# The last two stages of a four-layer gated block: first loads issued a stage earlier, first norms in the tail, statistics in eights

## The chip, the core and the metric

The kernel runs on one core of a Trainium2 chip. A core has five engines that matter here: TensorE (PE, matrix products and transposes into PSUM), VectorE (DVE), ScalarE (ACT), GpSimd (POOL) and SyncE (SP), which here only issues transfers. Each runs its own list of instructions in order and waits for others on semaphores. The metric is the device time of one execution in microseconds (us); lower is better.

## The reference, cut to what matters

`x` is 32 batches of 112 rows of 256. Four layers follow each other, each of an attention over a context of 375 rows and of a feed-forward part, both gated by a tanh and added to `x`. The change touches the last three parts: the ternary layer of layer 2, the masked attention and the routed layer of layer 3.

```python
# x (32, 112, 256), ctx (32, 375, 256), mask (32, 112, 375) of 0 and 1
x = x + tanh(g_ffn[2])   * ternary(_layernorm(x), ternary_weight, bias, act_scale)
x = x + tanh(g_xattn[3]) * masked(_layernorm(x), ctx, ctx, mask, gamma, beta)
x = x + tanh(g_ffn[3])   * routed(_layernorm(x), router_w, router_b, expert_weights)

def masked(q, k, v, mask, gamma, beta):
    logits = einsum('bsd,btd->bst', q, k) / sqrt(256)
    logits = where(mask == 0, -9e15, logits)
    x = einsum('bst,btd->bsd', softmax(logits), v)
    return _layernorm(x) * gamma + beta

def routed(tokens, router_w, router_b, expert_weights):       # 8 experts, the best 2 are used
    probs = softmax(einsum('bsh,eh->bse', tokens, router_w) + router_b)
    top_p, top_i = top_k(probs, 2)
    w = top_p / (sum(top_p) + 1e-10)
    y_all = einsum('nh,ehd->ned', tokens, expert_weights)      # every expert for every row
    return sum of w * y_all[top_i], divided by the clipped sum of w
```

## The kernel before

All of `x` stays in SBUF (`x_sb`) from the first layer to the last; the layers are blocks that follow one another, and at the end of a block every engine waits for the others. In the trace the ternary layer lies at 2764.9 to 2835.2 us, the masked attention at 2835.2 to 2960.4 and the routed layer at 2960.4 to 3235.7. The order of the instructions on each engine is written out by hand.

**Ternary layer** (`ternary_layer`, L2735). SP issues eight blocks of the context, `ctx_sb`, for the next stage (L2755) and has nothing else to do there.

**Masked attention** (`masked_attention`, L622 on). One pass of the loop for each of 32 batches, and three more to drain. PE: two transposes of the normed `x` (`transpose_xn`, L854), two matmuls with the transposed context `ctx_t` (`scores`, L864), three transposes of the probabilities two passes later (L873) and three matmuls with the context (`attend`, L884). ACT: copy of `xn_t` (L806), copy of `probs_t` (L820), the mask made into a summand (`add_mask`: `size` L795, `add` L799), the exponentials (L812), and the load of a context block whose buffer is free (`load_ctx`, L825); its list starts with the loads of gamma and beta. DVE: norm of the batch four ahead (L727), `kept` (L736, scores plus summand), `probs` with the top of a row (L740), statistics, and the adds to `x_sb` (L760). POOL: gain (L703), normalisation of the output and beta. SP: masks for two batches at a time in three buffers (L668), `ctx_t` in four buffers (L673), late in the stage the eight matrices of experts (`we`, L681). At the end POOL raises the variances of the first eight batches plus epsilon to the power -1/2 (`routed_scales(0)`, L568) and with that the block ends. `load_ctx` also runs for the last eight batches, which reload context blocks 0 to 7 that nobody reads.

**Routed layer** (`routed_layer`, L2866 on). The batches are routed in three groups, 0 to 7, 8 to 15 and 16 to 31 (`ROUTES`). For a group: statistics of `x` (`routed_statistics`, L550 and L553), rstd on POOL (`routed_scales`), norm on DVE (L2924) into eight buffers `xn`, two transposes on PE (L3042), copy on ACT (L3031), two matmuls with the router (L3053) and `route_group` on DVE, some 24 small instructions that choose the two experts and their weights. Then for each pair of batches PE runs 16 matmuls with a 128x512 operand (32 records in the trace) (`experts`, L3065) into five banks of PSUM, and DVE adds each result, weighted, to `x_sb` (`add_experts`, L2992). What DVE and PE do for the next group is written between the pairs of the present one: statistics after pair 0 of a group, eight norms after the second, the other eight norms (if there are sixteen) and `route_group` after the third; PE has its transposes and logits after the second pair, and the second eight after the third.

## Time and profile before

| | us |
|---|---|
| median of three runs | 3272.77 |
| lowest and highest of them | 3262.78, 3273.53 |
| the profiled execution | 3237.5 |
| its span | 3235.7 |
| granted clock over the span, share of full | 0.96 |
| masked attention | 125.2 |
| routed layer | 275.3 |

PE is busy for 94% of the span, DVE 62%, ACT 45%, POOL 19%. The rows are in the section below, taken from three views: the table by stretches (busy time of each engine in a stretch), and the timeline (one line for a run of like instructions of one engine, with start, busy time, and in brackets the longest wait ahead and what ended it). In names of tiles `ps` is PSUM.

### The profile page before, as it was taken

What the parts mean: (1) busy time and instruction counts of PE and PEld (TensorE: products, weight loads), DVE (VectorE), ACT (ScalarE), POOL (GpSimd) and SP (SyncE); (2) the same over time, 40 slices, a digit from 0 to 9 for tenths busy, and PEclk for the clock granted to TensorE, in tenths of its full rate; (3) what the DMA queues carried; (4) which work ended last, traced back from release to release, by engine and by line L of the source; (5) the groups of instructions that cost most, each with busy time, mean ns of one, the idle gap of its engine ahead of it and who ended that gap; (6) DMA issues with size and microseconds to landing.
All of it is one profiled execution on the core that took longest, in us unless ns stands there. A gap on an engine that the chain in (4) does not pass through costs nothing. (4 is left out here: it accounts for less than half of the span.)

```text
span 3235.7 us, 61226 instructions
## 1 busy us (share of the span) xinstructions
PE 3050.7 (94%) x23544; PEld 2320.6 (72%) x23544; DVE 2016.5 (62%) x4398; ACT 1460.9 (45%) x2829; POOL 622.7 (19%) x891
## 2 busy tenths in 40 slices
PE   7987699989999999999999999799999999889899
PEld 6875456667689999999999998566666666565343
DVE  3446111126677877788787877566666666687654
ACT  3431111115545555555555555466666666353000
POOL 3535200025200121023021200212112120054000
PEclk8987799989999999999999999899999999898999
DMA  7642133237500000000000000100000000184000
GB/s 235 194 166 67 60 117 117 79 120 233 185 25 1 2 2 1 2 2 2 1 1 2 2 1 1 30 21 21 16 21 21 18 18 11 40 259 149 12 15 17
DMA packets 76098, 184.95 MB, mean 57 GB/s; under 512 B 12214, under 2 KB 18739, under 8 KB 75477
## 3 DMA queue, kind: packets, MB, share of 16 engines
q1 hardware_dynamic: 57876, 137.60, 13.2%
q10 hardware_dynamic: 11600, 28.68, 2.8%
q0 software_dynamic: 6336, 14.76, 1.6%
q8 instruction: 193, 3.16, 0.4%
q14 instruction: 93, 0.75, 0.1%
HBM read 153.40 MB, written 27.79 MB: 56 GB/s over the span
## 5 line engine op out<-in xcount | busy, mean ns | idle before, releaser
L2525 ACT ACTIVATE probs<-probs,neg_top 112x375 f32<-112x375 f32 x512 | 281.8, 599 | 12.8 <-DVE neg_top L2448 11.7
L2448 DVE CUSTOM_DVE_ANT_0 probs<-ps,add 112x375 f32<-112x375 f32 x512 | 250.2, 546 | 55.7 <-PE ps L2599 54.7
L3065 PE MATMUL ps<-we,xn_t 128*112 128x512 f32 x512 | 233.3, 618 | 10.8 <-DVE x_sb L2992 10.8
L1385 DVE TENSOR_TENSOR hidden<-gated,ps 128x512 f32<-128x512 f32 x64 | 44.0, 688 | 303.1 <-PE ps L1428 303.1
L2005 DVE TENSOR_REDUCE top<-ps 112x16 f32<-112x1792 f32 x96 | 194.3, 2024 | 58.3 <-PE ps L2243 56.7
L2626 PE MATMUL ps<-ident,probs 112*125 112x112 f32 x1536 | 222.5, 281 | 2.8 <-DVE probs_t L2455 2.8
L2455 DVE COPY probs_t<-ps 125x336 f32<-125x336 f32 x256 | 128.9, 503 | 151.4 <-PE ps L2626 151.4
L2626 PEld LDWEIGHTS ps<-ident,probs 112*125 112x125 f32 x1536 | 189.7, 188 | 30.7 <-issue 18.9
L3065 PEld LDWEIGHTS ps<-we,xn_t 128*112 128x112 f32 x512 | 94.0, 185 | 147.0 <-issue 118.9
L2021 DVE TENSOR_TENSOR probs<-probs,inv_sum 112x1792 f32<-112x1792 f32 x96 | 197.2, 2054 | 3.3
L2017 DVE TENSOR_REDUCE row_sum<-probs 112x16 f32<-112x1792 f32 x96 | 193.9, 2020 | 4.3 <-ACT probs L2129 4.3
L2009 DVE TENSOR_TENSOR probs<-ps,top 112x1792 f32<-112x1792 f32 x96 | 194.3, 2024 | 3.3
L2211 PE MATMUL ps<-ident,probs 112*112 112x112 f32 x1536 | 180.6, 260 | 7.8 <-ACT probs_t L2124 7.3
L2226 PE MATMUL ps<-nodes,wq 128*128 128x224 f32 x768 | 182.8, 361 | 4.3
L2124 ACT ACTIVATE probs_t<-ps 112x896 f32<-112x896 f32 x192 | 176.1, 917 | 15.3 <-PE ps L2211 4.1
L2202 PE MATMUL ps<-wv,nodes 128*112 128x256 f32 x768 | 181.4, 379 | 0.0
L2211 PEld LDWEIGHTS ps<-ident,probs 112*112 112x112 f32 x1536 | 162.9, 134 | 25.6 <-issue 7.9
L2228 PE MATMUL ps<-att_t,wo 128*128 128x224 f32 x768 | 177.3, 353 | 0.0
L2182 PE MATMUL ps<-nodes,wkh 128*128 128x224 f32 x768 | 171.9, 367 | 0.0
L2992 DVE SCALAR_TENSOR_TENSOR x_sb<-ps,weight,x_sb 112x256 f32<-112x256 f32 x256 | 110.1, 478 | 98.8 <-PE ps L3065 98.8
L1998 DVE COPY v<-ps 112x512 f32<-112x512 f32 x96 | 66.4, 691 | 168.5 <-PE ps L2202 168.5
L2531 ACT ACTIVATE probs_t<-ps 125x336 f32<-125x336 f32 x256 | 115.5, 451 | 117.7 <-PE ps L2626 116.2
(401 smaller groups left out, 6316.1 us busy)
## 6 DMA issues: line engine op xcount, KB each, us to landing
ctx_t<-in_ctx_T_dram SPq DMA_DIRECT2D x96, 375.0 KB, 3.8
ctx_sb<-in_ctx_dram ACTq DMA_DIRECT2D x72, 384.0 KB, 4.2
ctx_sb<-in_ctx_dram SPq DMA_DIRECT2D x32, 384.0 KB, 4.6
ctx_sb<-in_ctx_T_dram SPq DMA_DIRECT2D x32, 375.0 KB, 3.0
queue<-zeros SPq DMA_DIRECT2D x32, 256.0 KB, 4.7
rows<-queue SPq DMA_DIRECT2D x16, 512.0 KB, 4.9
outputs<-out SPq DMA_DIRECT2D x16, 512.0 KB, 2.9
mask_in<-in_mask_BxSxS_fk_dram SPq DMA_DIRECT2D x16, 328.1 KB, 5.8
```

Of the source, the lines that this page charges most:

```text
L2005: dve.tensor_reduce(top[:, :, :], scores, AX.X, ALU.max).then_inc(s["top_done"], 1)
L2009: dve.tensor_tensor(probs[:, m % 2, :, :, :], scores, top[:, :, :].unsqueeze(3).broadcast_to([S, 4, PAIR * HQ, S]), ALU.subtract).then_inc ...
L2017: dve.tensor_reduce(row_sum[:, :, :], p, AX.X, ALU.add).then_inc(s["sum_done"], 1)
L2021: dve.tensor_tensor(p, p, inv_sum[:, :, :].unsqueeze(3).broadcast_to([S, 4, PAIR * HQ, S]), ALU.mult).then_inc(s["probs_normed"], 1)
L2202: mm = pe.matmul(k.ps[0:S, ODD, b * D:(b + 1) * D], node_v[:, i, b * S:(b + 1) * S], w.wv[:, c, i, :], start=i == 0, stop=i == DC - 1)
L2211: mm = pe.transpose(k.ps[0:S, PT + h // 4, h % 4 * S:(h % 4 + 1) * S], probs[:, m % 2, h % 4, b * HQ + h // 4, :], k.ident[0:S, 0:S])
L2226: pe.matmul(k.ps[:, ODD, a * PS:(a + 1) * PS], w.wq[:, c, i, cut], node_q[:, i, :], start=i == 0, stop=False)
L2228: mm = pe.matmul(k.ps[:, ODD, a * PS:(a + 1) * PS], w.wo[:, c, i, cut], att_t[:, i, :], start=False, stop=i == DC - 1)
L2448: dve.tensor_tensor_reduce(out=probs[:, u, h, :], in0=k.ps[0:S, SCORE + h, 0:L], in1=add[:, j % 2, :], scale=1.0, scalar=BIG, op0=ALU.add, ...
L2525: act.activation(probs[:, u, h, :], probs[:, u, h, :], ACT.Exp, bias=neg_top[:, u, h:h + 1], scale=-1.0).then_inc(s["probs_done"], 1)
L2626: mm = pe.transpose(k.ps[0:KR, PT + h % 2, r * S:(r + 1) * S], probs[:, n % 3, h, r * KR:(r + 1) * KR], k.ident[0:S, 0:S])
L3065: mm = pe.matmul(k.ps[0:S, Y + at % YB, :], xn_t[:, j + u, c, :], r.we[:, c, e:e + TWO, :].rearrange("p e d -> p (e d)"), start=c == 0, st ...
```

## The change

Four things are changed; nothing of what is computed is.

- The first four blocks of `ctx_t`, the first three blocks of masks, gamma and beta are issued by SP in the ternary layer, ahead of the eight context blocks (before: by SP and ACT at the start of the masked stage). Their tiles therefore live longer. ACT copies the first `xn_t` before it makes the first mask into a summand. The eight reloads that nobody reads are dropped.
- In the masked stage the statistics for the first eight routed batches lie in passes 20 to 27 instead of 22 to 29; POOL computes rstd at pass 29 and a shift (minus mean times rstd) at pass 30, both instead of a rstd behind its loop.
- The first eight norms of the routed layer are done on ACT (Identity, scale rstd, bias shift) in the tail of the masked stage, and the first eight pairs of transposes, copies and logits follow there. The routed layer starts with `route_group(0)` and the first experts.
- Inside the routed layer statistics, rstd and norms come in eights: DVE does statistics of the second eight after pair 0, norms after pair 1, `route_group(1)` after pair 2, statistics of the third eight after pair 3, their norms and the statistics of the fourth after pair 4, the last norms after pair 5, `route_group(2)` after pair 6. PE has the transposes and logits of the second, third and fourth eight after pairs 2, 5 and 6.

```diff
-    if j not in ROUTES:
+    if j % NB:
...
-def routed_scales(k, r, pool, g):
-
-    cut = slice(ROUTES[g], ROUTES[g + 1])
-    pool.wait_ge(r.mean_done, ROUTES[g + 1])
+def routed_scales(k, r, pool, h):
+
+    cut = slice(NB * h, NB * (h + 1))
+    pool.wait_ge(r.mean_done, NB * (h + 1))
     pool.tensor_scalar(r.var_eps[:, cut], r.mean_var[:, cut, 1], LN_EPS, None, ALU.add).then_inc(r.eps_added, 1)
-    pool.wait_ge(r.eps_added, g + 1)
-    pool.tensor_tensor(r.rstd[:, cut], r.var_eps[:, cut], k.neg_half[0:S, 0:ROUTES[g + 1] - ROUTES[g]], ALU.pow).then_inc(r.rstd_done, 1)
+    pool.wait_ge(r.eps_added, h + 1)
+    pool.tensor_tensor(r.rstd[:, cut], r.var_eps[:, cut], k.neg_half[0:S, 0:NB], ALU.pow).then_inc(r.rstd_done, 1)
...
+def first_routed_shifts(k, r, pool):
+
+    cut = slice(0, NB)
+    pool.tensor_scalar(r.neg_mean[:, cut], r.mean_var[:, cut, 0], -1.0, None, ALU.mult).then_inc(r.means_negated, 1)
+    pool.wait_ge(r.means_negated, 1)
+    pool.wait_ge(r.rstd_done, 1)
+    pool.tensor_tensor(r.shift[:, cut], r.neg_mean[:, cut], r.rstd[:, cut], ALU.mult).then_inc(r.shifts_done, 1)
+
+
+def first_routed_norm(k, r, act, j):
+
+    act.wait_ge(r.shifts_done, 1)
+    act.activation(r.xn[:, j, :], batch(k.x_sb, j), ACT.Identity, bias=r.shift[:, j:j + 1], scale=r.rstd[:, j:j + 1]).then_inc(r.normed, 1)
+
+
+def routed_transpose(k, r, pe, j):
+
+    pe.wait_ge(r.normed, j + 1)
+    if j >= 2:
+        pe.wait_ge(r.xt_copied, j - 1)
+    for a in range(DC):
+        mm = pe.transpose(k.ps[:, R_XT + j % 2, a * S:(a + 1) * S], r.xn[:, j % NB, a * P:(a + 1) * P], k.ident[0:S, 0:S])
+    mm.then_inc(r.transposed, 1)
+
+
+def routed_copy(k, r, act, j):
+
+    act.wait_ge(r.transposed, j + 1)
+    act.activation(r.xn_t[:, j, :, :], k.ps[:, R_XT + j % 2, 0:DC * S].rearrange("p (a t) -> p a t", a=DC), ACT.Copy).then_inc(r.xt_copied, 1)
+
+
+def routed_logits(k, r, pe, j, at):
+
+    pe.wait_ge(r.xt_copied, j + 1)
+    if j == 0:
+        pe.wait_ge(r.router_loaded, 32)
+    for c in range(DC):
+        mm = pe.matmul(k.ps[0:S, R_LOGITS, at:at + E3], r.xn_t[:, j, c, :], r.rw_t[:, c, :], start=c == 0, stop=c == DC - 1)
+    mm.then_inc(r.logits_done, 1)
...
+                for j in range(CT, B):
+                    sp.wait_ge(s["scores_done"], j - CT + 1)
+                    load_masked_ctx_t(k, e, sp, j)
+                    if j % 2 == 1 and MR <= j // 2 + 1 < B // 2:
+                        sp.wait_ge(s["sized"], 2 * (j // 2 + 1 - MR + 1))
+                        load_masked_mask(k, e, sp, j // 2 + 1)
                     if j >= B - 2 * E3 and j % 2:
                         i = (j - B + 2 * E3) // 2
                         sp.dma_start(r.we[:, :, i, :], k.inputs["L3_ffn_expert_weights"][i]).then_inc(r.experts_loaded, 16)
                 for j in range(NB):
-                    sp.wait_ge(ctx_loaded[j], 16 * (B // NB))
+                    sp.wait_ge(ctx_loaded[j], 16 * (B // NB - 1))
...
-                routed_scales(k, r, pool, 0)
-                pool.wait_ge(r.rstd_done, 1)
+                    if j == B - 3:
+                        routed_scales(k, r, pool, 0)
+                    if j == B - 2:
+                        first_routed_shifts(k, r, pool)
...
-                    if B - NB - 2 <= j < B - 2:
-                        i = j - (B - NB - 2)
+                    if B - NB - 4 <= j < B - 4:
+                        i = j - (B - NB - 4)
                         dve.wait_ge(s["residual_done"], i + 1)
                         routed_statistics(k, r, dve, i)
-                    if j == B - 2:
+                    if j == B - 4:
...
                 def load_ctx(j):
                     act.wait_ge(s["att_done"], j - NB + 1)
-                    act.dma_start(k.ctx_sb[:, j % NB, :, :], k.inputs["ctx_1024"][j % B]).then_inc(ctx_loaded[j % NB], 16)
-
-                act.dma_start(gamma[:, :], row(k.inputs["L3_xattn_gamma"]).partition_broadcast(S)).then_inc(s["rows_loaded"], 16)
-                act.dma_start(beta[:, :], row(k.inputs["L3_xattn_beta"]).partition_broadcast(S)).then_inc(s["rows_loaded"], 16)
+                    act.dma_start(k.ctx_sb[:, j % NB, :, :], k.inputs["ctx_1024"][j]).then_inc(ctx_loaded[j % NB], 16)
+
                 act.dma_start(r.rw_t[:, :, :], k.inputs["L3_ffn_router_w"]).then_inc(r.router_loaded, 16)
                 act.dma_start(r.rb[:, :], row(k.inputs["L3_ffn_router_b"]).partition_broadcast(S)).then_inc(r.router_loaded, 16)
                 act.wait_ge(s["masked_ready"], 1)
+                copy_xn(0)
                 add_mask(0)
-                copy_xn(0)
                 for j in range(B + LAG):
                     if j + 1 < B:
                         copy_xn(j + 1)
                     if 0 <= j - 2 < B:
...
                         copy_probs_t(j - 2)
+                    if j == B:
+                        for i in range(0, 4):
+                            first_routed_norm(k, r, act, i)
+                    if j == B + 1:
+                        routed_copy(k, r, act, 0)
+                        routed_copy(k, r, act, 1)
+                        for i in range(4, NB, 2):
+                            first_routed_norm(k, r, act, i)
+                            first_routed_norm(k, r, act, i + 1)
+                            routed_copy(k, r, act, i - 2)
+                            routed_copy(k, r, act, i - 1)
+                        routed_copy(k, r, act, NB - 2)
+                        routed_copy(k, r, act, NB - 1)
                     if j + 1 < B:
...
-                    if 0 <= j - LAG < B:
+                    if 0 <= j - LAG < B - NB:
                         load_ctx(j - LAG + NB)
...
+                    if j == B + 1:
+                        pe.wait_ge(s["xn_t_copied"], B)
+                        pe.wait_ge(s["kept_done"], B)
+                        routed_transpose(k, r, pe, 0)
+                        routed_transpose(k, r, pe, 1)
                     if j < B:
                         scores(j)
                     if 0 <= j - 2 < B:
                         attend(j - 2)
+                for j in range(2, NB, 2):
+                    routed_transpose(k, r, pe, j)
+                    routed_transpose(k, r, pe, j + 1)
+                    for i in (j - 2, j - 1):
+                        routed_logits(k, r, pe, i, i * E3)
+                for i in (NB - 2, NB - 1):
+                    routed_logits(k, r, pe, i, i * E3)
...
+                for j in range(MASKED_CT):
+                    load_masked_ctx_t(k, e, sp, j)
+                for q in range(MASKED_MR):
+                    load_masked_mask(k, e, sp, q)
+                sp.dma_start(e.gamma[:, :], row(k.inputs["L3_xattn_gamma"]).partition_broadcast(S)).then_inc(e.rows_loaded, 16)
+                sp.dma_start(e.beta[:, :], row(k.inputs["L3_xattn_beta"]).partition_broadcast(S)).then_inc(e.rows_loaded, 16)
                 for j in range(NB):
                     sp.dma_start(k.ctx_sb[:, j, :, :], k.inputs["ctx_1024"][j]).then_inc(ctx_loaded[j], 16)
...
-                for g in range(1, GROUPS):
-                    routed_scales(k, r, pool, g)
+                for h in range(1, B // NB):
+                    routed_scales(k, r, pool, h)
...
+                def group_statistics(h):
+                    for i in range(NB * h, NB * (h + 1)):
+                        routed_statistics(k, r, dve, i)
+                    last_routed_mean(k, r, dve, NB * (h + 1) - 1)
+
+                def group_norms(h):
+                    for i in range(NB * h, NB * (h + 1)):
+                        norm(i)
+
                 route_group(0)
...
-                    start, ahead = ROUTES[g], ROUTES[g + 2] - ROUTES[g + 1] if g + 1 < GROUPS else 0
-                    for j in range(start, ROUTES[g + 1], 2):
-                        if ahead and j - start == 2:
-                            for i in range(ROUTES[g + 1], ROUTES[g + 1] + XN):
-                                norm(i)
-                        if ahead and j - start == 4:
-                            for i in range(ROUTES[g + 1] + XN, ROUTES[g + 2]):
-                                norm(i)
+                    for j in range(ROUTES[g], ROUTES[g + 1], 2):
                         add_experts(j)
-                        if ahead and j - start == 0:
-                            for i in range(ROUTES[g + 1], ROUTES[g + 2]):
-                                routed_statistics(k, r, dve, i)
-                            last_routed_mean(k, r, dve, ROUTES[g + 2] - 1)
-                        if ahead and j - start == 4:
-                            route_group(g + 1)
+                        if j == 0:
+                            group_statistics(1)
+                        elif j == 2:
+                            group_norms(1)
+                        elif j == 4:
+                            route_group(1)
+                        elif j == 6:
+                            group_statistics(2)
+                        elif j == 8:
+                            group_norms(2)
+                            group_statistics(3)
+                        elif j == 10:
+                            group_norms(3)
+                        elif j == 12:
+                            route_group(2)
...
-                    for j in range(ROUTES[g], ROUTES[g + 1]):
-                        act.wait_ge(s["transposed"], j + 1)
-                        act.activation(xn_t[:, j, :, :], k.ps[:, XT + j % 2, 0:DC * S].rearrange("p (a t) -> p a t", a=DC), ACT.Copy).then_inc(s["xt_copied"], 1)
+                    for j in range(max(ROUTES[g], NB), ROUTES[g + 1]):
+                        routed_copy(k, r, act, j)
                     act.wait_ge(s["exps_ready"], g + 1)
...
+                def route_batches(h):
+                    for j in range(NB * h, NB * (h + 1)):
+                        routed_transpose(k, r, pe, j)
+                        if j > NB * h:
+                            route(j - 1)
+                    route(NB * (h + 1) - 1)
...
+                for j in range(0, B, 2):
+                    experts(j)
+                    if j == 4:
+                        route_batches(1)
+                    elif j == 10:
+                        route_batches(2)
+                    elif j == 12:
+                        route_batches(3)
```

**Where it moves instructions, first on SP** at the turn from the ternary layer to the masked stage. Before (the branch of L2751 ends the ternary layer):

```order
L2752 UNCONDITIONAL_BRANCH
L2755 DMA ctx_sb<-in_ctx_dram 128x768 x8
L2751 UNCONDITIONAL_BRANCH
L663 UNCONDITIONAL_BRANCH
L668 DMA mask_in<-in_mask_BxSxS_ik_dram 112x750
L673 DMA ctx_t<-in_ctx_T_dram 128x750 x2
```

After:

```order
L2836 UNCONDITIONAL_BRANCH
L676 DMA ctx_t<-in_ctx_T_dram 128x750 x4
L670 DMA mask_in<-in_mask_BxSxS_ik_dram 112x750 x3
L2842 DMA gamma<-in_L_xattn_gamma_dram 112x256
L2843 DMA beta<-in_L_xattn_beta_dram 112x256
L2845 DMA ctx_sb<-in_ctx_dram 128x768 x8
L2835 UNCONDITIONAL_BRANCH
L730 UNCONDITIONAL_BRANCH
L676 DMA ctx_t<-in_ctx_T_dram 128x750 x2
```

Nine transfers have moved across the end of the ternary block and stand ahead of its eight.

**PE in the tail of the masked stage.** Before:

```order
L884 MATMUL ps<-ctx_sb,probs_t 112x256 x3
L873 MATMUL ps<-ident,probs 125x112 x3
L884 MATMUL ps<-ctx_sb,probs_t 112x256 x3
L662 UNCONDITIONAL_BRANCH
L3035 UNCONDITIONAL_BRANCH
L3042 MATMUL ps<-ident,xn 128x112 x4
L3053 MATMUL ps<-rw_t,xn_t 112x8 x2
...
L3053 MATMUL ps<-rw_t,xn_t 112x8 x4
L3065 MATMUL ps<-we,xn_t 112x512 x32
```

After (L593 is the routed transpose, L609 the logits, L945 and L956 are the L873 and L884 of before, L3147 is L3065):

```order
L945 MATMUL ps<-ident,probs 125x112 x3
L593 MATMUL ps<-ident,xn 128x112 x4
L956 MATMUL ps<-ctx_sb,probs_t 112x256 x3
L593 MATMUL ps<-ident,xn 128x112 x4
L609 MATMUL ps<-rw_t,xn_t 112x8 x4
L593 MATMUL ps<-ident,xn 128x112 x4
L609 MATMUL ps<-rw_t,xn_t 112x8 x4
L593 MATMUL ps<-ident,xn 128x112 x4
L609 MATMUL ps<-rw_t,xn_t 112x8 x8
L729 UNCONDITIONAL_BRANCH
L3131 UNCONDITIONAL_BRANCH
L3147 MATMUL ps<-we,xn_t 112x512 x48
```

The transposes of batches 0 and 1 stand ahead of `attend(31)`, the other six and the logits behind it, still inside the block, and the first experts come in a piece of three pairs (48) where it was two (32). The trace has two records for each of these instructions.

**DVE in the routed layer**, from the adds of batches 0 and 1 to the second route. Before:

```order
L2992 SCALAR_TENSOR_TENSOR x_sb<-ps,weight,x_sb 112x256 x16
L550 BN_STATS stats<-x_sb 112x6 x2
...
L559 BN_AGGR mean_var<-stats 112x2
L2924 TENSOR_SCALAR xn<-x_sb,mean_var,rstd 112x256 x8
L2992 SCALAR_TENSOR_TENSOR x_sb<-ps,weight,x_sb 112x256 x32
L2931 TENSOR_TENSOR logits<-ps,rb 112x64
```

After (L551, L560, L3012, L3080 and L3019 are the L550, L559, L2924, L2992 and L2931 of before):

```order
L3080 SCALAR_TENSOR_TENSOR x_sb<-ps,weight,x_sb 112x256 x16
L551 BN_STATS stats<-x_sb 112x6 x2
...
L560 BN_AGGR mean_var<-stats 112x2
L3080 SCALAR_TENSOR_TENSOR x_sb<-ps,weight,x_sb 112x256 x16
L3012 TENSOR_SCALAR xn<-x_sb,mean_var,rstd 112x256 x8
L3080 SCALAR_TENSOR_TENSOR x_sb<-ps,weight,x_sb 112x256 x16
L3019 TENSOR_TENSOR logits<-ps,rb 112x64
```

Sixteen adds now stand between the statistics and the norms.

## Rows read from the trace of the kernel before

**Rows 1.** Table by stretches, the routed stage: start and end, length, busy (xcount)

```profile
2960.40:3235.70 275.30, 258.67 (x704) 118.29 (x704) 152.01 (x498) 12.04 (x35) 5.11 (x4) 0.93 0.05 14
```

**Rows 2.** Timeline, opening of the masked stage: start, busy, engine, line [wait before]

```profile
2835.82 0.74 PE L854 MATMUL ps<-ident,xn 112*128 112x112 f32 x4 [2.16 <-DVE xn L727]
...
2839.94 0.52 ACT L795 ACTIVATE size<-mask_in 112x375 f32<-112x375 int32 x1 [11.44 <-DMA mask_in<-in_mask_BxSxS_ik_dram]
...
2841.00 0.58 ACT L806 ACTIVATE xn_t<-ps 128x224 f32<-128x224 f32 x2
...
2841.79 2.81 PE L864 MATMUL ps<-ctx_t,xn_t 128*112 128x375 f32 x4 [5.23 <-DMA ctx_t<-in_ctx_T_dram]
2841.87 0.35 DVE L769 TENSOR_SCALAR gamma<-gamma,tg 112x256 f32<-112x256 f32 x1 [3.01 <-DMA beta<-in_L_xattn_beta_dram]
...
2844.70 0.55 DVE L736 SCALAR_TENSOR_TENSOR kept<-add,ps 112x375 f32<-112x375 f32 x1 [2.22 <-issue]
```

**Rows 3.** Masked stage, a full pass by stretches, then timeline rows of DVE

```profile
2902.00:2905.40 3.40, 3.40 (x17) 2.33 (x16) 3.26 (x11) 2.27 (x7) 1.74 (x4) 1.00 0.91 289
...
2895.74 0.80 DVE L740 CUSTOM_DVE_ANT_0 probs<-kept,add 112x375 f32<-112x375 f32 x1
...
2939.07 0.42 DVE L550 BATCH_NORM_STATS2 stats<-x_sb 112x6 f32<-112x256 f32 x1
```

**Rows 4.** Timeline, from the masked to the routed stage

```profile
2953.07 0.45 ACT L820 ACTIVATE probs_t<-ps 125x336 f32<-125x336 f32 x1 [2.15 <-PE ps L873]
...
2953.62 1.52 PE L884 MATMUL ps<-ctx_sb,probs_t 125*112 125x256 f32 x6 [0.59 <-issue]
...
2957.47 1.73 POOL L568 TENSOR_TENSOR rstd<-var_eps,neg_half 112x8 f32<-112x8 f32 x1
...
2960.43 2.67 DVE L2924 TENSOR_SCALAR xn<-x_sb,mean_var,rstd 112x256 f32<-112x256 f32 x8 [2.77 <-PEq L631]
...
2969.78 2.03 PE L3065 MATMUL ps<-we,xn_t 128*112 128x512 f32 x2
```

**Rows 5.** Timeline of ACT in the ternary layer

```profile
2768.06 0.64 ACT L2781 ACTIVATE steps_t<-ps,scale 128x448 f32<-128x448 f32 x1
2768.59 1.08 ACT L2774 ACTIVATE normal<-x_sb,shift,gain 112x256 f32<-112x256 f32 x2
```

**Rows 6.** Timeline of DVE and PE, routed stage, around the waits

```profile
2987.57 0.74 DVE L550 BATCH_NORM_STATS2 stats<-x_sb 112x6 f32<-112x256 f32 x2
...
2995.60 4.79 DVE L2992 SCALAR_TENSOR_TENSOR x_sb<-ps,weight,x_sb 112x256 f32<-112x256 f32 x12
...
2996.92 5.40 PE L3065 MATMUL ps<-we,xn_t 128*112 128x512 f32 x12 [1.99 <-DVE x_sb L2992]
...
3034.58 27.72 PE L3065 MATMUL ps<-we,xn_t 128*112 128x512 f32 x64 [1.33 <-DVE x_sb L2992]
...
3054.94 0.74 DVE L550 BATCH_NORM_STATS2 stats<-x_sb 112x6 f32<-112x256 f32 x2
...
3067.38 3.61 DVE L2992 SCALAR_TENSOR_TENSOR x_sb<-ps,weight,x_sb 112x256 f32<-112x256 f32 x9
...
3068.69 8.03 PE L3065 MATMUL ps<-we,xn_t 128*112 128x512 f32 x12 [6.39 <-DVE x_sb L2992]
```

**Rows 7.** Table by stretches, routed stage: the column behind POOL is the granted clock

```profile
2960.80:2969.70 8.90, 8.72 (x48) 8.35 (x48) 2.30 (x8) 2.86 (x8) 0.00 (x0) 0.50 0.01 3
2969.70:2976.50 6.80, 6.80 (x12) 2.77 (x12) 5.57 (x42) 0.26 (x1) 0.00 (x0) 0.61 0.00 0
3001.70:3008.80 7.10, 6.84 (x50) 6.10 (x48) 1.27 (x3) 2.75 (x8) 0.00 (x0) 0.78 0.12 35
3068.60:3075.40 6.80, 6.71 (x10) 2.69 (x11) 4.01 (x11) 0.00 (x0) 0.00 (x0) 0.60 0.00 0
3098.10:3104.00 5.90, 5.90 (x54) 5.08 (x52) 1.27 (x3) 2.86 (x8) 0.00 (x0) 1.00 0.15 42
3104.00:3110.80 6.80, 6.80 (x15) 2.79 (x15) 5.84 (x57) 0.31 (x1) 0.00 (x0) 0.75 0.00 1
```

112 lines of the change are left out of this document (40 added, 72 removed).

## The prediction, made before the changed kernel was run

> **What bounds the kernel now.** I read the table by stretches first. In the routed stage PE is busy for 258.7 of 275.3 us and every other engine far less [rows 1]: 512 records of expert matmuls, one after the other, set its length. Whatever delays the first of them, makes one wait, or lets one run at half clock is time on the path. Next came the timelines at the two seams. The masked stage opens with nothing to work on: the transposes of batch 0 end at 2836.56, but ACT waits 11.44 us for its first mask, PE 5.23 us for ctx_t and DVE 3.01 us for beta; the first `kept` starts at 2844.70 [rows 2]. At the other seam `attend(31)` ends on PE at 2955.14, POOL's power ends at 2959.20, DVE starts the first routed norm at 2960.43, and the first expert matmul starts only at 2969.78 [rows 4]. Inside the routed stage the timeline of PE shows three waits for DVE's adds, of 1.99, 1.33 and 6.39 us [rows 6]. The granted clock comes last: 1.00 is 2.4 GHz and 0.50 is 1.2 GHz, and the stage has several stretches between the two [rows 7].
>
> **The sum is made against the profiled execution,** 3237.5 us (span 3235.7 and 1.8 around it). The median of the three runs, 3272.8, stands 35.3 above it. I take the same microseconds off the median. A measurement of this kernel can tell some 0.3% (9.8 us) from no change.
>
> **A. First loads a stage earlier: 4.9 us gained.** Four ctx_t, three mask blocks, gamma and beta are issued in the ternary layer ahead of the eight ctx blocks. They queue ahead of those on SP; nothing there waits for them, and the first ctx block is read two passes into the masked stage. With everything resident, scores(0) needs the transposes (2836.56) and one ACT copy, which now stands ahead of the mask on ACT. Two copies take 0.58, so I count 0.35 and start at 2836.9. Before, `kept` came 2.91 after the start of scores(0) (2841.79 to 2844.70) at low clock; so it comes at 2839.8 [rows 2]. What is late next is DVE, which scales gamma and beta after its first norms. I allow it 0.3 us either way for an upper bound of 5.2. The lower bound is the whole wait staying in another place, 0.
>
> **B. Routed statistics two passes earlier: 1.2 us lost.** Around 2902 to 2905 DVE is busy for 3.26 of 3.40 and so sets the pass; there, one more bn_stats (0.42) that used to lie in passes 28 and 29 now lies in 20 and 21, with masked statistics beside it. Two passes grow by some 0.45 and nothing comes back, since PE is as full there: 0.9. POOL gets rstd of the first eight inside its loop at pass 29 (two instructions, 1.73 of it the power) and two small ones for the shift at pass 30. Behind them stand `add_beta` and the gain for DVE. POOL's slack covers most of that, but DVE's `probs` takes 0.80 where POOL is at work late, [rows 3], and I put POOL's part in that at some 0.25, an estimate; 0.3 for it. Bounds 0 and 2.0.
>
> Rule against row: that 0.80 shows DVE and POOL in each other's way. The Trainium skill (SBUF — State Buffer, Who interferes with whom) says that a DVE instruction with two SBUF inputs contends with a GpSimd instruction that reads SBUF, over a shared port. By its rule all 2.3 us that are added on POOL could stand against DVE, and the sum would be 2.0 us less; the row allows at most its own 0.80 in such a pass.
>
> **C. First norms, transposes and logits in the masked tail: 6.8 us gained.** Eight norms go to ACT, which idles there: two of the same shape take 1.08 in the ternary layer [rows 5], so 0.54 each. Four stand between the copies of probs_t(30) and probs_t(31); ACT is done with them at about 2953.1, when probs_t(31) was copied anyway (2953.07), so `attend(31)` is not late. PE transposes batches 0 and 1 ahead of it. Behind 2955.14 are left six transposes and eight logits, some 7.3 batches' worth. Eight batches take 5.90 at full clock and 8.90 at half [rows 7]: 5.4 to 8.1, PE ends at 2960.5 to 2963.2, and I take 2961.8, since PE has been thinly busy and I expect it to fall to half on the way. DVE's last add and POOL are done by then, so PE is what closes the block. From POOL's end to DVE's start the turn took 1.23 [rows 4], so the experts start at 2963.0 instead of 2969.78: 6.8, bounds 5.4 and 8.1. The turn also no longer has eight reloads of ctx (nobody reads them) to wait out; they landed about when POOL ended, so this is worth nothing apart.
>
> Nothing in the trace loads an activation table when Identity and Copy take turns [rows 5]. The Trainium skill (ScalarE: Activation LUTs, What ACT_TABLE_LOAD costs) puts a switch of table sets at about 2.66 us; it counts Identity into every set, so it predicts none here either, and were it otherwise, an estimate by that page would be 5.3 less in the sum.
>
> **C'. A shorter spell at half clock at the start: 0.9 us gained.** The first 6.8 us of experts ran at a mean of 0.61, a loss of 0.39 × 6.8 = 2.7. After a batch of transposes without a stall ahead of it the same length ran at 0.75, a loss of 1.7 [rows 7]. PE now comes from a 1.2 us gap, not from 5.8 us. Bounds 0 and 2.7.
>
> **D. Stalls on DVE: 9.7 us gained.** DVE leaves its adds at 2987.57 and is back at 2995.60, 8.03 later, and PE stalls 1.99; it leaves at 3054.94, is back at 3067.38, 12.44 later, and PE stalls 6.39 [rows 6]. Both differences are 6.04: with five banks of PSUM, DVE may be away 6.0 us before PE waits. The change cuts the absences. Eight statistics at 0.37 to 0.42 each are 3.0 to 3.3 [rows 3, 6]; eight norms take 2.67 [rows 4]. The longest absence is norms of the third eight with statistics of the fourth, 5.7 to 6.0: just under. POOL's power is no longer waited for, since it runs under a pair of experts. The second route (the 1.33) moves behind the transposes, so PE spends the first part of it on work that fills no bank, and an absence of 7.4 (6.04 + 1.33) fits. So 1.99 + 1.33 + 6.39 = 9.7. Lower bound 8.7, if the tight one fails by half and another slips.
>
> **E. Half clock behind the stalls: 3.9 us gained.** After the stall of 6.39 the clock was 0.60 for 6.8 us, a loss of 2.7. The first batch inside the stage took 7.10 at 0.78, behind a stall; the last 5.90 at 1.00, behind none [rows 7]: 1.2 more. Bounds 0 and 5.5 (the same again for the spell behind the batch).
>
> On this row and rule part: the spells follow stalls and runs of small matmuls. The Trainium skill (TensorE: Matmul & The Clock Gate, What's actually happening) says that half rate is the default and activity releases it, and calls the number of slow matmuls variable from run to run, 6 to 14 for one kernel; by that, C' and E could be anything in their bounds in a given run.
>
> **Sum:** 4.9 − 1.2 + 6.8 + 0.9 + 9.7 + 3.9 = 25.0 us. 3272.8 − 25.0 = **3247.8 us**; a profiled execution by the same count is 3212.5. The bounds that can go together give a gain of 17 to 31.
>
> **Rivals.**
> - The clock gives nothing back: PE still falls to half behind each run of transposes, for as long. For it: every batch but the last was followed or crossed by such a stretch. Against it: the last batch ran wholly at 1.00. C' and E go: 20.2 gained, 3252.6.
> - The tail is the new wait: ACT's norms wait for POOL's shift, hold the copy of probs_t(31) behind them by up to 2.2 us, and all the rest runs at half: PE ends at 2965.4, experts start at 2966.6, C is 3.2 and C' 0. Gain 20.5, 3252.3. For it: in the tail POOL, ACT and PE pass the work on in single steps. Against it: POOL was busy for 1.74 of a pass of 3.40 [rows 3].
> - The change doesn't do what it says: the early loads are not what `kept` waits for, and A is 0, because the chain of norm, transpose, copy and the scaling of gamma takes as long. Gain 20.1, 3252.7. Against it: the rows name three DMA waits and nothing else in that place.
> - Slower: PE enters the experts at half clock and stays there. A matmul takes 27.72 / 64 = 0.43 us at full [rows 6] and 0.86 at half. Fifty-eight more at half eat the whole gain, 81 make it slower by over 0.3%; with the first four pairs (128 records) at half it is +55 − 25 = +30, 3302.8. For it: no stage between the ternary layer and the end would then rest PE long enough to matter, and the first stretch, behind a rest, had a mean of 0.61 over 6.8 us. Against it: in no stretch here does a dense run stay at half beyond some seven matmuls (a loss of 2.7 is 5.4 us at half).
> - All goes well, with full clock at both seams: gain 31, 3241.8.
>
> **How the numbers follow.** Forecast (gain 21 to 29) 0.50; clock 0.16; tail 0.12; loads without effect 0.06; all well 0.06; slower by over 0.3% 0.04; two or three of the middle ones at once, which leaves under 9.8 us, 0.06. So faster 0.90, same 0.06, slower 0.04. The range takes in the rivals at 3252 to 3253, the bounds of the terms, and half of the 10.7 us between the three runs shown: 3238 to 3260. It leaves out the two last cases and some of the edges, 0.2 at most.
>
> **What would show it.** A: the first `kept` starts 4 to 5 us after the block begins, with no DMA named. B: two passes of 3.9 us at 20 and 21. C: the first expert matmul 5 to 6 us after the last add of the masked stage, PE closing the block. D: one wait of PE for DVE's adds is left, of about 1 us behind the sixteen-wide route, which the change leaves as it is. E: no stretch at 0.60 in the middle of the stage. Wrong would be: PE waiting again for adds of more than 2 us in all, ACT or POOL as the last to arrive in the tail, or more than 40 expert matmuls at half clock.

## The result and the profile after

| | before | after |
|---|---|---|
| median of six runs each, us | 3270.52 | 3243.97 |
| lowest, highest | 3262.78, 3275.62 | 3239.89, 3250.74 |
| span of the profiled execution | 3235.7 | 3242.6 |

The ratio is 0.9922, with a 95% interval of 0.9909 to 0.9934: 25.5 us faster, where 25.0 was forecast. The two medians are 26.6 apart. The one after is 3.8 below the 3247.8 of the forecast, in part because the median before fell by 2.3 when three more executions joined it. The two profiled executions say the opposite at first sight, 3242.6 after and 3235.7 before. They have to be set against each other from the first instruction that the change touches. The ternary layer's first transfer is issued at 2764.92 before and at 2797.49 after; up to there both run the same code, so these 32.6 us are no part of the change (the last section says with what they go). From there to the end it is 470.78 before and 445.11 after: 25.67 less. By stretches:

| stretch | before | after | gained | forecast |
|---|---|---|---|---|
| ternary layer | 70.32 | 70.30 | 0.0 | 0 |
| start of the masked stage to the first `kept` | 9.46 | 4.19 | 5.3 | 4.9 (A) |
| first `kept` to the end of `attend(31)` | 110.44 | 111.85 | −1.4 | −1.2 (B) |
| end of `attend(31)` to the first expert matmul | 14.64 | 6.10 | 8.5 | 6.8 (C) |
| first expert matmul to the last | 261.19 | 247.82 | 13.4 | 14.5 (C', D, E) |
| last expert matmul to the end | 4.73 | 4.85 | −0.1 | 0 |

The opening of the masked stage after the change, timeline (columns as in [rows 2]):

```profile
2868.38 0.73 PE L926 MATMUL ps<-ident,xn 112*128 112x112 f32 x4 [2.16 <-DVE xn L788]
...
2869.15 0.51 ACT L856 ACTIVATE size<-mask_in 112x375 f32<-112x375 int32 x1
...
2869.30 1.52 PE L936 MATMUL ps<-ctx_t,xn_t 128*112 128x375 f32 x4 [0.19 <-ACT xn_t L867]
...
2871.34 0.35 DVE L830 TENSOR_SCALAR gamma<-gamma,tg 112x256 f32<-112x256 f32 x1
...
2871.98 0.55 DVE L797 SCALAR_TENSOR_TENSOR kept<-add,ps 112x375 f32<-112x375 f32 x1
2872.29 1.71 POOL L751 TENSOR_TENSOR x_sb<-x_sb,beta 112x256 f32<-112x256 f32 x2
...
2872.56 0.86 DVE L801 CUSTOM_DVE_ANT_0 probs<-kept,add 112x375 f32<-112x375 f32 x1
...
2873.36 0.80 DVE L788 TENSOR_SCALAR xn<-x_sb,mean_var,rstd 112x256 f32<-112x256 f32 x1
```

No DMA ends a wait here any more, where three did [rows 2]. The stage begins at 2867.79 and `kept` comes at 2871.98, as soon as DVE has scaled beta. The last three rows are the price: POOL's first adds of beta run beside DVE's `probs` (0.86) and norm (0.80), which take 0.55 and 0.41 elsewhere.

The tail, timeline:

```profile
2981.76 0.45 ACT L881 ACTIVATE probs_t<-ps 125x336 f32<-125x336 f32 x1 [0.18 <-PE ps L945]
...
2982.31 1.52 PE L956 MATMUL ps<-ctx_sb,probs_t 125*112 125x256 f32 x6 [0.20 <-issue]
...
2986.50 2.50 PE L609 MATMUL ps<-rw_t,xn_t 128*112 128x8 f32 x16
...
2989.93 8.63 PE L3147 MATMUL ps<-we,xn_t 128*112 128x512 f32 x15 [0.93 <-PEq L703]
```

ACT copied probs_t(31) 0.18 after its transposes, so its four norms were not in the way. PE closes the block at 2989.0, and the first expert starts 0.93 later; before, the same turn held POOL's power, DVE's norms and a whole batch [rows 4].

Inside the routed stage, the timeline of PE and the longest absence of DVE:

```profile
3039.28 44.33 PE L3147 MATMUL ps<-we,xn_t 128*112 128x512 f32 x96
...
3071.09 2.66 DVE L3012 TENSOR_SCALAR xn<-x_sb,mean_var,rstd 112x256 f32<-112x256 f32 x8
...
3073.68 0.74 DVE L551 BATCH_NORM_STATS2 stats<-x_sb 112x6 f32<-112x256 f32 x2
...
3076.90 4.78 DVE L3080 SCALAR_TENSOR_TENSOR x_sb<-ps,weight,x_sb 112x256 f32<-112x256 f32 x12
...
3089.22 15.66 PE L3147 MATMUL ps<-we,xn_t 128*112 128x512 f32 x32
...
3110.84 126.90 PE L3147 MATMUL ps<-we,xn_t 128*112 128x512 f32 x288
```

None of these rows has a wait ahead. The three of [rows 6] are gone, and a fourth of 1.11 that stood ahead of the last 268 records. DVE is away from 3071.09 to 3076.90, 5.81 us, just under the 6.04 of the prediction. What stayed is the clock. The grouped view of the expert matmuls, before and then after (busy, mean ns, idle before and its releaser):

```profile
L3065 PE MATMUL ps<-we,xn_t 128*112 128x512 f32 x512 | 233.3, 618 | 10.8 <-DVE x_sb L2992 10.8
```

```profile
L3147 PE MATMUL ps<-we,xn_t 128*112 128x512 f32 x512 | 230.3, 613 | 0.9 <-PEq L703 0.9
```

Pieces at full clock took 5.40 for 12 records, 27.72 for 64 and 115.27 for 268: 0.429 a record and some 0.24 once for each piece. By that the 512 records and the pieces (eight before, four after) need 221.7 and 220.7 us. What is over is half clock: 11.6 before, 9.6 after. The table by stretches, for the 6.8 us behind the tail and behind each batch of transposes and logits (clock behind POOL's column, as in [rows 7], which has three such rows of before), first the two of before that are missing there, then all four after:

```profile
3008.80:3015.60 6.80, 6.80 (x14) 2.86 (x14) 1.68 (x4) 0.00 (x0) 0.00 (x0) 0.72 0.00 0
3081.90:3088.70 6.80, 6.80 (x11) 2.64 (x12) 0.83 (x3) 0.00 (x0) 0.00 (x0) 0.58 0.00 0
```

```profile
2989.90:2996.70 6.80, 6.77 (x12) 2.76 (x13) 5.70 (x43) 0.26 (x1) 0.00 (x0) 0.71 0.01 4
3039.30:3046.10 6.80, 6.80 (x10) 2.62 (x11) 5.63 (x43) 0.26 (x1) 0.00 (x0) 0.57 0.00 0
3089.30:3096.10 6.80, 6.80 (x13) 2.65 (x13) 1.75 (x4) 0.00 (x0) 0.00 (x0) 0.75 0.00 0
3110.80:3117.60 6.80, 6.80 (x11) 2.68 (x11) 5.86 (x57) 0.31 (x1) 0.00 (x0) 0.56 0.01 4
```

And the three batches themselves, after:

```profile
3033.16:3039.28 6.12, 5.77 (x49) 5.08 (x48) 1.27 (x3) 2.75 (x8) 0.00 (x0) 0.92 0.14 40
3083.45:3089.22 5.77, 5.40 (x50) 4.65 (x48) 4.22 (x11) 2.75 (x8) 0.00 (x0) 1.00 0.15 43
3104.72:3110.84 6.12, 5.75 (x49) 5.00 (x48) 1.27 (x3) 2.75 (x8) 0.00 (x0) 0.93 0.13 37
```

### The profile page after: what moved, and what is told of

Its sections match the earlier page's. It is cut to its first block and busy times, and to the rows that moved or that the text cites. A ratio compares the mean times of both kernels' runs of the same rounds, so it can differ in the third digit from the quotient of the medians.

```text
span 3242.6 us, 61215 instructions
## 1 busy us (share of the span) xinstructions
PE 3045.5 (94%) x23544; PEld 2317.1 (71%) x23544; DVE 2015.1 (62%) x4390; ACT 1462.9 (45%) x2837; POOL 622.2 (19%) x895
## 5 line engine op out<-in xcount | busy, mean ns | idle before, releaser
L2609 ACT ACTIVATE probs<-probs,neg_top 112x375 f32<-112x375 f32 x512 | 281.8, 599 | 12.9 <-DVE neg_top L2532 11.7
L3147 PE MATMUL ps<-we,xn_t 128*112 128x512 f32 x512 | 230.3, 613 | 0.9 <-PEq L703 0.9
L3147 PEld LDWEIGHTS ps<-we,xn_t 128*112 128x112 f32 x512 | 93.4, 184 | 134.7 <-issue 119.0
L2213 ACT ACTIVATE probs<-probs 112x1792 f32<-112x1792 f32 x96 | 162.9, 1697 | 8.3 <-DVE probs L2093 8.1
```

The lines of the kernel that those rows point to most:

```text
L2609: act.activation(probs[:, u, h, :], probs[:, u, h, :], ACT.Exp, bias=neg_top[:, u, h:h + 1], scale=-1.0).then_inc(s["probs_done"], 1)
L3147: mm = pe.matmul(k.ps[0:S, Y + at % YB, :], xn_t[:, j + u, c, :], r.we[:, c, e:e + TWO, :].rearrange("p e d -> p (e d)"), start=c == 0, st ...
```

## The experiments

All times of stretches are from the profiled execution of each kernel; ratios are against the kernel before, run beside it on the same chip. The first three kernels are the changed one with the rest put back to what it was before, and two things of the changed kernel stay in all three: POOL raises its variances by eight, and PE waits for its two semaphores ahead of the logits in the other order.

**The first loads alone.** The kernel before, with

```diff
+                for j in range(MASKED_CT):
+                    load_masked_ctx_t(k, e, sp, j)
...
+                copy_xn(0)
                 add_mask(0)
-                copy_xn(0)
```

> The kernel before with the first loads alone a stage earlier (four ctx_t, three masks, gamma, beta; the copy of xn_t ahead of the mask), and without the eight unread reloads. Theory from the two traces: the first kept starts 4.2 us after the masked stage begins instead of 9.5, with no DMA named, the rest of the stage and the ternary layer keep their lengths: 5.3 us less, ratio 0.998. Rival: the early transfers are paid elsewhere (a longer ternary layer, or attend(0) waiting for its context block, which now queues behind nine transfers): the kept is early and the stage ends no earlier, ratio 1.000. Second rival: kept is early by less, since the chain of norms and scaling on DVE takes its place: 3 us or under.

Ratio 0.9979 (0.997 to 0.9988). The first `kept` came 4.19 after the stage began, 5.27 earlier, and the loop was 0.69 longer, in the first pass (3.70 between the first two `kept` instead of 2.99). So A is worth 4.6. The routed stage of this kernel was to be as before, but POOL's scales were left by eight, and that showed something. Before, and then in this kernel:

```profile
3064.79 2.68 DVE L2924 TENSOR_SCALAR xn<-x_sb,mean_var,rstd 112x256 f32<-112x256 f32 x8 [3.40 <-POOL rstd L568]
```

```profile
3059.47 5.40 PE L3123 MATMUL ps<-we,xn_t 128*112 128x512 f32 x12 [2.99 <-DVE x_sb L3054]
```

Before, DVE's norms waited 3.40 for one power over sixteen batches. With two powers over eight each they do not wait, DVE is away 9.04 instead of 12.44, and PE waits 2.99 instead of 6.39. The stretch of the experts is 4.0 shorter: 3.4 by this and the rest by what the clock and the batches did. With the 4.6 that makes this kernel's 8.4, where 5.3 was expected.

The first 6.8 us of its experts bear on C':

```profile
2963.00:2969.80 6.80, 6.80 (x14) 2.88 (x14) 5.55 (x42) 0.26 (x1) 0.00 (x0) 0.77 0.00 0
```

Here the experts follow a batch at the start of the stage, as before, and yet the clock was 0.77 and not 0.61.

**The eights alone.** The kernel before, with the changed order on DVE, PE and POOL in the routed stage:

```diff
+                            group_statistics(2)
+                        elif j == 8:
+                            group_norms(2)
+                            group_statistics(3)
+                        elif j == 10:
+                            group_norms(3)
+                        elif j == 12:
+                            route_group(2)
```

> The kernel before with statistics, scales and norms of the routed stage in eights and the PE batches at the changed places, alone; loads and tail as before, the first eight norms and transposes at the start of the routed stage, the reloads kept. Theory: all four waits of PE for DVE's adds go (1.99 + 1.33 + 6.39 + 1.11 = 10.8 us) and with them the one spell at half clock that followed the wait of 6.39 (2.9 us); the spells behind batches of transposes stay. 13.7 us less from the first expert matmul to the last, ratio about 0.996. Rival (the clock gives nothing back): the spell comes at some other place and the gain is the 10.8 alone. Rival: without the tail the first waits come back, under 8 us.

Ratio 0.9965 (0.9952 to 0.9979); experts in 248.01 instead of 261.19, 13.2 less. All four waits were to go, and one is left, 1.12 behind the sixteen-wide route. The changed kernel had none there, yet its last 288 records took 126.90, and so they did before with a wait of 1.11: where the spell at half clock behind the batch is longer by 1.1, PE is too slow to fill the banks and the wait is hidden in it. That wait was not removed but traded.

**The tail alone.** The kernel before with statistics two passes earlier, POOL's scales and shifts in the loop, and norms, transposes and logits in the tail:

```diff
+                    if j == B:
+                        for i in range(0, 4):
+                            first_routed_norm(k, r, act, i)
...
+                    if j == B + 1:
+                        pe.wait_ge(s["xn_t_copied"], B)
+                        pe.wait_ge(s["kept_done"], B)
+                        routed_transpose(k, r, pe, 0)
+                        routed_transpose(k, r, pe, 1)
```

> The kernel before with the tail alone: statistics two passes earlier, POOL's scales and shifts in its loop, eight norms on ACT, transposes, copies and logits in the masked stage, no reloads; loads at the start of the stage and the routed stage's order as before (POOL's scales by eight). Theory: from the last attend to the first expert matmul 6.1 us instead of 14.6, less 1.4 us for a longer loop: 7.1 us less; the first spell at half clock is 0.9 us shorter; the three waits of PE stay, 8.0 us less in all, ratio 0.9975. Rival: the 1.4 us is no cost of the tail but of the early loads (the loop then starts at another clock), and this kernel gains 9.4. Rival: the full clock in the tail comes from the early loads, and the tail here costs 2 us more.

Ratio 0.9963 (0.995 to 0.9977). The loop was 0.67 longer, in passes 20 to 22 only (3.75 and 3.81 where 3.42 and 3.43 stood), the turn took 5.25 instead of 14.64, and the experts 257.0 instead of 261.19, with POOL's smaller powers as above: 12.9 less in all, where 8.0 was expected. The wait of 2.99 brought a spell at half clock here (the twelve records behind it took 8.32), which it did not in the kernel with the loads alone (5.40). The table by stretches for the tail, this kernel and then the changed one:

```profile
2947.23:2951.55 4.32, 4.32 (x45) 4.14 (x42) 1.97 (x5) 2.68 (x8) 1.06 (x2) 1.00 0.00 0
```

```profile
2983.83:2989.00 5.17, 5.17 (x45) 4.98 (x42) 1.98 (x5) 2.68 (x8) 1.06 (x2) 0.81 0.00 0
```

At full clock the six transposes and eight logits that are left behind `attend(31)` take 4.32; at a mean of 0.81 they take 5.17. Why the tail has full clock without the early loads and not with them is open. The parts add up: 0.69 and 0.67 are the 1.4 of the loop. The three kernels gained 8.4, 13.0 and 12.9; the 4.0 and 4.2 that the first and the third gained among the experts are in the second's 13.0 already, and without them the sum is 26.1 for the 25.7 of the whole.

**Idle work on DVE.** The changed kernel, with

```diff
+                        elif j == 18:
+                            for i in range(21):
+                                dve.bn_stats(idle[:, i, :], batch(k.x_sb, 0))
+                        elif j == 26:
+                            for i in range(21, 53):
+                                dve.bn_stats(idle[:, i, :], batch(k.x_sb, 0))
```

> The changed kernel with useless statistics on DVE, far from any batch of transposes: 21 bn_stats behind the adds of batches 18 and 19 (an absence of some 8.2 us) and 32 behind those of 26 and 27 (12.5 us). Their result is used by nothing. Theory that DVE may be away 6.0 us with five banks: PE waits 2.2 and 6.5 us. Theory on the clock: a half-clock spell that costs 2.9 us follows the long wait and none follows the short one; the piece from the first of the two to the end is 8.7 + 2.9 = 11.6 us longer. Rival: a spell needs the small matmuls of a batch, and none follows either wait: 8.7. Rival: any wait of 2 us brings a spell: 14.5.

```profile
3122.28 6.95 DVE L3124 BATCH_NORM_STATS2 idle<-x_sb 112x6 f32<-112x256 f32 x21
...
3129.14 4.78 DVE L3081 SCALAR_TENSOR_TENSOR x_sb<-ps,weight,x_sb 112x256 f32<-112x256 f32 x12
...
3130.45 55.19 PE L3154 MATMUL ps<-we,xn_t 128*112 128x512 f32 x128 [0.81 <-DVE x_sb L3081]
...
3178.28 10.54 DVE L3127 BATCH_NORM_STATS2 idle<-x_sb 112x6 f32<-112x256 f32 x32
...
3188.73 3.60 DVE L3081 SCALAR_TENSOR_TENSOR x_sb<-ps,weight,x_sb 112x256 f32<-112x256 f32 x9
...
3190.04 5.35 PE L3154 MATMUL ps<-we,xn_t 128*112 128x512 f32 x6 [4.40 <-DVE x_sb L3081]
```

```profile
3130.40:3137.20 6.80, 6.75 (x16) 2.93 (x17) 5.27 (x13) 0.00 (x0) 0.00 (x0) 1.00 0.00 0
3190.00:3196.80 6.80, 6.76 (x10) 2.69 (x11) 4.08 (x10) 0.00 (x0) 0.00 (x0) 0.62 0.00 0
```

Without semaphores a bn_stats took 0.33, not 0.39, so the absences were 6.86 and 10.45 and the waits shorter than the 2.2 and 6.5 expected. The rule holds all the better: 6.86 − 0.81 = 6.05 and 10.45 − 4.40 = 6.05, beside the 6.04 and 6.05 from which it was taken. Behind the short wait PE stayed at full clock; behind 4.40, with no batch near, it had 6.8 us at 0.62. So a wait alone can bring a spell. Whether one of 2 us does in this place was not tried, since the short wait came out at 0.81.

**Four banks.** `LOGITS, Y, YB = R_LOGITS, 3, 4` in the changed kernel.

> The changed kernel with four banks of PSUM for the experts' results in place of five. Theory: DVE may be away 6.04 us less the 1.72 that PE takes for one result, 4.3 us. Absences of 3.2 and 2.7 stay free; the one of 5.81 (norms of the third eight, statistics of the fourth) makes PE wait 1.5; the two routes inside the stage lose what the batch of transposes does not cover, about 1.7 more each than now. Some 5 us longer from the first expert matmul to the last. Rival: the 6.04 is DVE's own time to catch up and not a count of banks, then there is no wait.

```profile
3068.64 2.66 DVE L3012 TENSOR_SCALAR xn<-x_sb,mean_var,rstd 112x256 f32<-112x256 f32 x8
...
3074.44 3.80 DVE L3080 SCALAR_TENSOR_TENSOR x_sb<-ps,weight,x_sb 112x256 f32<-112x256 f32 x9
...
3075.74 4.55 PE L3147 MATMUL ps<-we,xn_t 128*112 128x512 f32 x10 [1.47 <-DVE x_sb L3080]
```

An absence of 5.80 now costs 1.47: 4.33 are free, 1.72 less than with five banks, and 1.72 is the time of one result on PE (four records). Behind the sixteen-wide route PE waited 2.94, behind the other not at all, where 1.7 each was expected; 4.7 us longer in all. So the 6.04 counts banks.

**The changed kernel again**, on the chip of the next kernels.

> The changed kernel again, beside the others of this set. Ratio to before 0.992 as in its first timing. By the parts alone it would be: loads 4.6 us, tail 8.7, eights 10.8 plus what the clock gives, 26 us. Which of its batches of transposes are followed by a half-clock spell, and how long each is, differs from its first profile if the spells are chance in the single case; the waits of PE stay at none, save that of 1.1 behind the sixteen-wide route, which comes only where the spell behind the batch is short.

Ratio 0.9934 (0.9919 to 0.9949), and every stretch within 0.2 us of the first profile, the spells too: the pieces behind the batches took 44.39, 15.66 and 126.90, where they took 44.33, 15.66 and 126.90. The kernel with idle work, on another chip, has 44.33 and 15.66 as well. They are no chance of the single run.

**Batches spread among the experts.** The changed kernel, with the following, and with DVE's route split in two halves behind two pairs and its statistics of the third eight behind pair 1:

```diff
                             mm.then_inc(s["experts_done"], 1)
+                            if h:
+                                i = NB * h + e // TWO * 2 + u
+                                if i == NB * h:
+                                    routed_transpose(k, r, pe, i)
+                                else:
+                                    route(i - 1)
+                                if i + 1 < NB * (h + 1):
+                                    routed_transpose(k, r, pe, i + 1)
+                                else:
+                                    route(i)
...
-                    experts(j)
-                    if j == 4:
-                        route_batches(1)
+                    experts(j, {4: 1, 10: 2, 12: 3}.get(j))
```

> The changed kernel with the transposes and logits of the second, third and fourth eight spread among the expert matmuls of one pair each (one batch behind each of the eight results) in place of three runs of some 6 us; DVE's route is split in two halves behind two pairs, so that no absence is over 6 us, and the statistics of the third eight stand two pairs earlier. Theory: the half-clock spells behind the batches (2 to 3 us each, three of them) come from PE having little to do in a run of small matmuls that wait for ACT; with the run gone the spells go, and part of the waits for ACT: 8 us from spells and 3 from the batches, 11 less from the first expert matmul to the last than the 247.8 of the changed kernel, ratio 0.9965 against it. Rival: the spells come at intervals whatever PE does between, and only the 3 us are gained. Rival: each small matmul between large ones costs a refill, and it is slower by up to 3.

```profile
3016.00:3034.00 18.00, 18.00 (x81) 9.73 (x80) 12.69 (x42) 2.82 (x8) 1.92 (x2) 1.00 0.05 14
3034.00:3040.80 6.80, 6.80 (x17) 2.82 (x17) 4.67 (x21) 0.26 (x1) 0.00 (x0) 1.00 0.12 34
3080.00:3098.00 18.00, 18.00 (x80) 9.87 (x79) 9.27 (x24) 2.75 (x8) 0.00 (x0) 1.00 0.05 14
3098.10:3104.90 6.80, 6.80 (x18) 2.94 (x18) 5.53 (x30) 0.31 (x1) 0.00 (x0) 1.00 0.12 35
```

The clock is 1.00 among and behind the batches. From first expert to last it took 237.09, 10.7 less than the changed kernel: some 7.6 from the three spells (0.43, 0.25 and 0.44 of 6.8), some 3.8 from batches that no longer wait for ACT nor run partly at half clock, less one wait of 0.67. The changes on DVE gain nothing by themselves, since PE had no wait for DVE that could go. Ratio to before 0.9888 (0.9865 to 0.9911), where the changed kernel beside it has 0.9934: this version beats both.

**Gamma and beta scaled later.** The changed kernel with DVE's two scalings behind its first norm of the loop; run twice, and once together with the spread batches.

```diff
-                dve.wait_ge(e.rows_loaded, 32)
...
                         norm(j + XR)
+                    if j == 0:
+                        dve.wait_ge(e.rows_loaded, 32)
```

> The changed kernel with DVE's scaling of gamma and beta moved behind its first kept, probs and norm of the masked stage, so that POOL's first adds of beta (1.71 us), which wait for it, no longer run beside probs and the norm. Theory: early loads lose 0.7 us in the first pass because POOL's adds slow two DVE instructions (probs 0.86 instead of 0.55, norm 0.80 instead of 0.41). Here they take 0.55 and 0.41 again and the second kept comes 0.7 us sooner after the stage's start, 7.2 instead of 7.9. Rival: the first DVE instructions of a stage are slow for another reason, and both keep their lengths.

> The kernel with the batches spread among the experts and, besides, the scaling of gamma and beta moved behind DVE's first norm of the loop. From the first expert matmul to the last 237 us as with the spread alone. For the opening of the masked stage: if the half clock in which PE ran attend(0) in the run with the late scaling alone (2.45 us, and a third pass of 5.62 instead of 4.12) was chance, the passes are 3.6, 1.9, 4.1 here and kept(3) comes 0.7 us earlier after the stage's start than in the changed kernel; if the later scaling brings it, 5.6 comes again and the stage is 0.8 longer. Ratio to before 0.988 either way.

> The changed kernel with the late scaling of gamma and beta, a second look at the same program. If the half clock at attend(0) was chance, the third pass is 4.1 here in one of the two looks; if the order brings it, 5.6 in all three.

```profile
2865.88 0.55 DVE L801 CUSTOM_DVE_ANT_0 probs<-kept,add 112x375 f32<-112x375 f32 x1
...
2866.36 0.41 DVE L788 TENSOR_SCALAR xn<-x_sb,mean_var,rstd 112x256 f32<-112x256 f32 x1
...
2867.37 1.42 POOL L751 TENSOR_TENSOR x_sb<-x_sb,beta 112x256 f32<-112x256 f32 x2 [1.08 <-DVE beta L841]
...
2871.44 2.45 PE L957 MATMUL ps<-ctx_sb,probs_t 125*112 125x256 f32 x6 [2.18 <-ACT probs_t L882]
```

```profile
2870.00:2875.00 5.00, 3.56 (x12) 2.90 (x13) 2.79 (x11) 3.32 (x10) 2.80 (x5) 0.69 0.30 96
```

`probs` takes 0.55 again and the norm 0.41, and the second `kept` came 0.7 sooner after the stage's start (7.2 instead of 7.9). So the 0.7 that the early loads lost was DVE and POOL in each other's way. But then PE runs `attend(0)` at half clock (2.45 for what takes 1.55), the third pass is 5.62 instead of 4.12, and more than all is given back: the fourth `kept` comes 0.8 later after the stage's start than in the changed kernel. It was so in all three runs (5.62, 5.61, 5.61), so the order brings it and no chance. The kernel with both edits has a ratio of 0.9888 (0.9871 to 0.9906), no better than the spread alone.

## Why the prediction was right, and where not

**A held, 4.9 against 5.3** (its upper bound was 5.2), and what was late next was DVE's scaling, as named. Its price was not in the sum: 0.7 in the first pass. This is the contention that I weighed against the trace in B and put at 0.3, on POOL's work at passes 29 and 30. There it cost nothing (2.94 and 3.27 both times), and here it cost 0.7. The Trainium skill (SBUF — State Buffer, Who interferes with whom) has a DVE instruction with two SBUF inputs contend with a GpSimd instruction that reads SBUF, and `tensor_scalar` with GpSimd where it runs in a two-port mode. `probs` has two SBUF inputs, and the kernel with the late scaling agrees: 0.55 instead of 0.86. The norm went from 0.80 to 0.41; whether it runs in a two-port mode no row shows.

**B: 0.7 against 1.2.** The two passes grew by 0.33 and 0.38, where 0.45 each was worked out (3.75 and 3.81, not the 3.9 named as a sign); the 0.3 for POOL was the contention put in the wrong place.

**C: 8.5 against 6.8,** outside its bounds of 5.4 to 8.1. The term that failed is the price of a batch, 5.90 at full clock for eight, taken from batches in which PE takes one batch at a time and waits for ACT's copy in each. In the tail it takes two batches' transposes, then two batches' logits: 4.3 at full clock. PE's expected fall to half came only in part (0.81), so it took 5.17 where 6.7 was forecast. The turn of the block then took 0.93 and not 1.2. PE did close the block, but the first expert came 3.6 us after DVE's last add, not 5 to 6.

**C': the number held, the reason did not.** In the first 6.8 us of experts the loss went from 2.7 to 2.0 (0.61 to 0.71): 0.7 against 0.9. The forecast put it down to a shorter gap ahead of PE. But the gap of 5.8 lay ahead of the batch, not of the experts, and the kernel with the loads alone, which kept gap and batch, lost only 1.6 (0.77). So what makes this spell shorter is open, and the agreement is luck.

**D: 9.7 was forecast and 10.8 of waits went,** of which 1.1 only changed its name (the wait behind the sixteen-wide route, which I expected to stay, hid in a longer spell). The rule of 6.04 us for five banks is the best part of the prediction: beside the two absences that it was taken from, two more and a count of banks bear it out. The forecast said that POOL's power would no longer be waited for, but not that this was 3.4 of the 6.39; the bracket of DVE's norm says so.

**E failed in half: some 1.9 against 3.9** (13.4 for the whole stretch, less 10.8 and 0.7). The spell behind the wait of 6.39 went: its twelve records had taken 8.03 where 5.40 is usual, 2.6 for the 2.7. The other 1.2, "the first batch ran at 0.78, behind a stall; the last at 1.00, behind none", was the step that failed: the batches now have no stall ahead and two of the three ran at 0.92 and 0.93, and behind each is a spell as before. All three batches take 18.0 us, where they took 17.6, and the spells behind them cost 7.6, where they cost 6.4. The sign that was named for E, no stretch at 0.60 in the middle of the stage, did not come: two are at 0.57 and 0.56. These spells follow the run of small matmuls, not the stall, as the rival that the clock gives nothing back had it for these; the spread kernel shows it. (At a clock of 1.00 a batch took 5.77 after and 5.52 before, and 5.77 again with the eights alone and with the tail alone. The order of PE's two waits ahead of the logits is a suspect, and no run separates it.) The Trainium skill (TensorE: Matmul & The Clock Gate, What's actually happening) has the number of slow matmuls vary from run to run of one kernel. Here it did not: two executions of the changed kernel agree within 0.13 us in every piece of the experts, and so do two of the one with the late scaling, on two chips. By the table, the measured terms stood above the forecast by 0.4 in A, 1.7 in C and 1.1 in D, and below it by 0.2 in B, 0.2 in C' and 2.0 in E, and 0.1 was lost at the end: 0.7 in all. The total is nearer than its terms deserve, and that is luck.

**The other rivals.** The tail as the new wait and the loads without effect are refuted by the rows above; the slower case, half clock kept through the experts, did not come: each spell lost 1.5 to 3.1 us, which is 3 to 6 us at half clock, in every run.

## What to carry to other kernels

Count what a consumer may be away in banks: here five banks bear 6.0 us and four 4.3 where the consumer had caught up before it left, and any work put between its steps should be cut to pieces below that, its waits on other engines included. Put small matmuls between large ones instead of in a run, and not only for the waits: here the spell at half clock behind a run cost 1.5 to 3.1 us and its own waits about one. Look at what a term rests on even where its number comes out: C' did, for another reason. Set two profiled executions against each other from the first instruction that differs.

## What the runs showed of the hardware that I had not expected

- Which waits of PE among experts were followed by half clock: behind 0.8, 1.1, 1.3, 1.5 and 2.9 (four banks) none; behind 2.0 none in two programs and one in a third, where the next 12 records took 7.10 instead of 5.4; behind 2.99 none in the kernel with the loads alone, but one in the kernel with the tail alone; behind 4.4 and 6.4 it came in the one case of each. What decides between 2.0 and 3.0 is open.
- Removing 0.7 us of DVE's time at the start of the masked stage made PE fall to half clock some 6 us later, in three runs of three. Why this order does it is open: PE waits 2.18 ahead of `attend(0)` there and 1.92 in the changed kernel, and no run changes that wait alone.
- The same code took 32.6 us longer up to the ternary layer in one profiled execution than in another, and this goes with the chip, not with the single execution. In the profiles whose chip is known the ternary layer starts at 2756.5 to 2763.2 on two chips (six profiles) and at 2791.4 to 2797.5 on a third (four), and the medians of the kernel before were 3231.4 and 3235.7 on the two and 3266.1 on the third. Most of it lies in the first layer, where POOL waits for DVE's places ahead of 64 indirect transfers: 42.6 us in all in the first profile of before, 66.7 in that of after, 36.6 to 41.7 on the two chips and 65.5 to 67.3 on the third. What makes the chips differ is open.
